# A chunk's gate and up halves handed over separately, and the low half of h subtracted on GpSimd

## The chip, the cores and the metric

The kernel runs on one core of a Trainium2 chip. The metric is the device time of one execution in microseconds (us), the median of several runs. The core has a matrix engine (TensorE, PE in the profile), VectorE (DVE), ScalarE (ACT), GpSimd (POOL) and a queue that issues transfers (SyncE, SP). Each engine takes its own instructions strictly in order; they meet only at semaphores.

## The reference, cut to what matters

```python
low, highs = x, []                                  # x: (2, 4096, 512)
for _ in range(2):                                  # two levels of a filter bank along the tokens
    highs.append(dwconv(low, g_filter)[:, ::2]); low = dwconv(low, h_filter)[:, ::2]
low = linear_attention(low, 16)
for h in reversed(highs):
    low = dwconv(repeat(low, 2), h_synth) + dwconv(repeat(h, 2), g_synth)
x = layernorm(x + layer_norm(x + low, gamma, beta))

gate = x @ (w_gate / 127).T                         # w_gate, w_up: (1536, 512)
up   = x @ (w_up / 127).T
h    = silu(gate) * up
x    = layernorm(x + h @ (w_down / 127).T)
```

The last four lines are the feed-forward part (FFN). Each float operand of its products is carried as two float16 halves: a high half, which is the value rounded to float16, and a low half, which is the value less its high half.

## The kernel before, in words

After an opening (the first analysis of the filter bank, up to 203 us of the span) the program runs eight iterations of 1024 tokens. An iteration does the FFN of its tokens in two blocks of 512 tokens (b is 0 or 1), and beside it, in small steps, the filter bank, the attention and the layer norms of the next iteration; iterations 0 to 2 also do a piece of the analysis of the second batch ("ANA"), and the last has no next one. The table `BESIDE` (line 66) says which step stands beside which chunk: `(b, k)` with k from 0 to 11 for the gate and up chunks, and from 12 to 15 for the four groups of tokens of the down product. On each engine the order is written out by these loops; nothing reorders it.

A chunk k is 128 of the 1536 hidden columns. For it

- PE (`gate_up`, L512 to L524) waits until the product of chunk k-2 has been formed (`h_mul`; that frees the PSUM buffers `ps_gu[k % 2]`), then runs 8 matmuls for gate and 8 for up, and signals once, `gu_ready`, after all 16.
- ACT (L752 to L759) waits for `gu_ready`, writes silu(gate) to `gate_s` (L754), does its "early" steps of the table, waits for the product, writes the high half `h_hi` (L758, a cast to float16), and does its "late" steps. The squares of the layer norms are among the late ones (`norm1q` L671, `normq` L677) and so is `normx` (L683).
- DVE (L1064 to L1080) waits for the silu, multiplies it by the up half, from PSUM, into `h_f` (L1070), does its steps of the table, waits for `h_hi` and writes the low half, `h_f - h_hi` (L1076, `hid<-h_f,hid` in the profile). For k = 0 the steps stand ahead of the product, for k = 11 after the low half.
- POOL has no part in a chunk. It does small steps of the layer norms on one value in each partition (`norm1` L795, `norm1q` L803 and L806, `norm2` L810, `normq` L816 to L821) and `xbeta` (L790), an addition of two SBUF tiles of 128x512.

The filter steps on DVE are `scalar_tensor_tensor` instructions, all recorded at L864: `low1` and `high1` are six of 514 elements and two short corrections of edges (L869), `synth1a` and `synth1b` five of 512, `synth2` eight of 257 and an edge. All their tensor operands lie in SBUF, as those of `norm2` (L1006, L1012) do. The product (L1070), `x_lo` (L1020), `att` (L941) and the residual `z` (L1088) read one operand from PSUM and one from SBUF.

The layer norm of a group t of 128 tokens goes round the engines: DVE `norm2` (L1006, L1012), then POOL L810, then ACT's square L677, then POOL L816 to L821, then ACT `normx` L683, then PE's transposes L507, ACT `x_hi` L688, and DVE `x_lo` L1020.

## Time and profile before

| | |
|---|---|
| median of 3 runs | 1384.56 us (1384.21, 1384.56, 1386.04) |
| profiled execution, first to last instruction | 1382.5 us |
| granted PE clock, mean | 0.971 of full; 1.00 in every stretch from 350 us to 1250 us |
| PE, DVE, ACT, POOL busy | 1245.5, 988.1, 688.8, 373.0 us |
| iterations 0 to 7 | from 203 us to the end; 155 us each for 1 and 2, 144.4 us each for 4, 5 and 6 |

The span is the profiled execution's own time; the median of the runs lies 2.1 us above it. A matmul of 512 columns is recorded with 380 ns, but at full clock one starts every 0.216 us, and its record overlaps the next one's; so an idle stretch of PE of g us in the profile stands for g + 0.16 us in which no matmul started. A chunk of 16 matmuls takes 3.46 us when nothing holds it.

### The profile page before, as it was taken

To read this page: it belongs to the slowest core of one execution; us is meant where nothing else is said; L and a number is where in the kernel's file an instruction comes from. 1 tells how busy PE (TensorE), PEld (TensorE's weight loads), DVE (VectorE), ACT (ScalarE), POOL (GpSimd) and SP (SyncE) were. 2 spreads that over 40 slices of the span, in tenths; PEclk is the share of its full clock that TensorE was granted. 3 is DMA by queue.
4 is the path that set the end of the run, shared out by engine and by line. 5 is a ranking of instruction groups with operands and counts; after the bars stand their busy time and mean duration, and the time that the engine had idled before them with its cause. 6 is when DMAs were issued, how large, how long until landed. Compare 5 with 4: busy or idle time off the path is not lost.

```text
span 1382.5 us, 18903 instructions
## 1 busy us (share of the span) xinstructions
PE 1245.5 (90%) x5920; PEld 629.5 (46%) x5920; DVE 988.1 (71%) x1913; ACT 688.8 (50%) x1384; POOL 373.0 (27%) x790
## 2 busy tenths in 40 slices
PE   3997039998999989998999999999999999999998
PEld 3885025444444444444544444444444444444443
DVE  2677938988688958988489738883898478854332
ACT  2663046345753466346753466346634664365432
POOL 2001033133423044223413143304321341234101
PEclk9998559999999999999999999999999999999999
DMA  8963033000520014000500041002200130010000
GB/s 262 285 238 123 0 123 108 23 24 24 176 77 31 0 55 147 20 23 24 176 16 31 8 148 30 31 1 84 100 23 8 53 122 23 15 38 24 16 16 31
DMA packets 48465, 95.20 MB, mean 69 GB/s; under 512 B 8448, under 2 KB 25088, under 8 KB 47376
## 3 DMA queue, kind: packets, MB, share of 16 engines
q1 hardware_dynamic: 48400, 94.42, 20.8%
q8 instruction: 30, 0.49, 0.1%
q14 instruction: 35, 0.29, 0.1%
HBM read 69.21 MB, written 25.19 MB: 68 GB/s over the span
## 4 chain that ended last, share of the span: by engine, by line
DVE 29%; PE 27%; issue 22%; ACT 12%; POOL 9%; SPq 0%; DMA 0%; DVEq 0%; POOLq 0%; ACTq 0%
DVE s_chan L864 6%; DVE h_f L1070 5%; DVE low L864 5%; PE ps_down L540 3%; PE ps_down L539 3%; PE ps_gate L522 3%; PE ps_gate L523 3%; PE ps_up L523 3%; PE ps_up L522 3%; DVE hid L1076 3%; POOL rs L819 3%; DVE h_mem L864 3%; PE ps_down L572 2%; ACT junk L671 2%; DVE l L864 2%
## 5 line engine op out<-in xcount | busy, mean ns | idle before, releaser
L522 PE MATMUL ps_gate<-x_hi,w 128*128 128x512 f16 x768 | 292.4, 381 | 27.5 <-DVE h_f L1070 25.4
L539 PE MATMUL ps_down<-w,hid 128*128 128x512 f16 x768 | 292.1, 380 | 0.1
L540 PE MATMUL ps_down<-w,hid 128*128 128x512 f16 x768 | 292.1, 380 | 0.0
L523 PE MATMUL ps_gate<-x_lo,w 128*128 128x512 f16 x768 | 292.0, 380 | 0.0
L522 PE MATMUL ps_up<-x_hi,w 128*128 128x512 f16 x768 | 291.1, 379 | 0.0
L523 PE MATMUL ps_up<-x_lo,w 128*128 128x512 f16 x768 | 291.1, 379 | 0.0
L758 ACT ACTIVATE hid<-h_f 128x512 f16<-128x512 f32 x192 | 121.0, 630 | 203.2 <-DVE h_f L1070 203.2
L1070 DVE SCALAR_TENSOR_TENSOR h_f<-ps_up,gate_s 128x512 f32<-128x512 f32 x192 | 131.7, 686 | 123.7 <-ACT gate_s L754 123.1
L1076 DVE TENSOR_TENSOR hid<-h_f,hid 128x512 f16<-128x512 f32 x192 | 139.3, 725 | 57.7 <-ACT hid L758 56.8
L754 ACT ACTIVATE gate_s<-ps_gate 128x512 f32<-128x512 f32 x192 | 112.1, 584 | 70.0 <-PE ps_up L523 69.8
L522 PEld LDWEIGHTS ps_gate<-x_hi,w 128*128 128x128 f16 x768 | 75.2, 98 | 124.9 <-DVE h_f L1070 42.2
L522 PEld LDWEIGHTS ps_up<-x_hi,w 128*128 128x128 f16 x768 | 75.2, 98 | 90.8 <-issue 0.3
L523 PEld LDWEIGHTS ps_up<-x_lo,w 128*128 128x128 f16 x768 | 75.1, 98 | 90.8 <-issue 0.3
L790 POOL TENSOR_TENSOR xt<-xt,beta_b 128x512 f32<-128x512 f32 x64 | 90.1, 1429 | 97.6 <-DMA xt<-x_tok 96.8
L539 PEld LDWEIGHTS ps_down<-w,hid 128*128 128x128 f16 x768 | 75.3, 98 | 86.8 <-DVE z L1088 3.5
L540 PEld LDWEIGHTS ps_down<-w,hid 128*128 128x128 f16 x768 | 75.3, 98 | 85.2 <-issue 1.1
L864 DVE SCALAR_TENSOR_TENSOR s_chan<-low,coef,s_chan 128x512 f32<-128x512 f32 x160 | 111.5, 748 | 1.1
L523 PEld LDWEIGHTS ps_gate<-x_lo,w 128*128 128x128 f16 x768 | 75.3, 98 | 78.7 <-issue 0.8
L795 POOL TENSOR_TENSOR rs<-rs,minus_part 128x1 f32<-128x1 f32 x64 | 21.2, 331 | 324.6 <-ACT x L666 324.6
L1020 DVE TENSOR_TENSOR x_lo<-ps_y,x_hi 128x512 f16<-128x512 f32 x64 | 43.9, 687 | 85.2 <-ACT x_hi L688 85.2
L746 ACT ACTIVATE z<-z,rs 128x512 f32<-128x512 f32 x64 | 52.0, 812 | 83.3 <-POOL rs L821 83.3
L741 ACT ACTIVATE junk<-z,rs 128x512 f16<-128x512 f32 x64 | 46.0, 718 | 89.9 <-POOL rs L839 89.9
(106 smaller groups left out, 1803.8 us busy)
## 6 DMA issues: line engine op xcount, KB each, us to landing
xa<-x_chan SPq DMA_DIRECT2D x32, 515.0 KB, 5.6
xb<-x_chan SPq DMA_DIRECT2D x8, 2060.0 KB, 8.9
xt<-x_tok SPq DMA_DIRECT2D x64, 256.0 KB, 2.6
out<-z SPq DMA_DIRECT2D x64, 256.0 KB, 2.0
hid<-weights SPq DMA_DIRECT2D x12, 768.0 KB, 6.7
q_in<-q_scratch SPq DMA_DIRECT2D x8, 518.0 KB, 8.5
h_in<-h_scratch SPq DMA_DIRECT2D x8, 518.0 KB, 9.5
h_scratch<-h SPq DMA_DIRECT2D x8, 512.0 KB, 9.2
```

The lines of the kernel that those rows point to most:

```text
L522: pe.matmul(ps_gu[k % 2][g][:, :], w, x1_hi[:, b, c, :], start=(c == 0), stop=False)
L523: mm = pe.matmul(ps_gu[k % 2][g][:, :], w, x1_lo[:, b, c, :], start=False, stop=(c == NC - 1))
L539: pe.matmul(ps_d[t % 2][:, :], h_hi[:, k, t * P:(t + 1) * P], w, start=(k == 0), stop=False)
L540: mm = pe.matmul(ps_d[t % 2][:, :], h_lo[:, k, t * P:(t + 1) * P], w, start=False, stop=(k == NH - 1))
L741: nc.scalar.activation(junk[:, :], z[:, t, :], ACT.Square, bias=rs3[:, t, 1:2], accum_out=rs3[:, t, 2:3]).then_inc(z_squares, 1)
L746: nc.scalar.activation(z[:, t, :], z[:, t, :], ACT.Identity, bias=rs3[:, t, 5:6], scale=rs3[:, t, 4:5]).then_inc(out_done, 1)
L754: nc.scalar.activation(gate_s[:, k % 2, :], ps_gu[k % 2][0][:, :], ACT.Silu, scale=WSCALE / X1_SCALE).then_inc(silu_done, 1)
L758: nc.scalar.activation(h_hi[:, k, :], h_f[:, k % 2, :], ACT.Copy).then_inc(hi_done, 1)
L790: nc.gpsimd.tensor_tensor(xt[:, t % 4, :], xt[:, t % 4, :], beta_b[:, :], ALU.add).then_inc(x_beta, 1)
L864: return V.scalar_tensor_tensor(out=acc, in0=src, scalar=coef[:, c, n:n + 1], in1=acc if add is None else add, op0=ALU.mult, op1=ALU.add)
L1070: V.scalar_tensor_tensor(out=h_f[:, k % 2, :], in0=ps_gu[k % 2][1][:, :], scalar=WSCALE * H_SCALE / X1_SCALE, in1=gate_s[:, k % 2, :], op0 ...
L1076: V.tensor_tensor(h_lo[:, k, :], h_f[:, k % 2, :], h_hi[:, k, :], ALU.subtract).then_inc(lo_done, 1)
```

## The change

Four things are changed together.

1. PE signals the gate half and the up half of a chunk apart (`gate_ready`, `up_ready`). Ahead of the gate half it waits for the silu of chunk k-2, ahead of the up half for the product of chunk k-2.
2. ACT's silu waits for `gate_ready`, and for the low half of chunk k-4.
3. The silu is written into `h_f`, a ring of four buffers, and DVE writes the product over it; `gate_s` is gone. DVE waits for the silu and for `up_ready`, and its steps of the table follow the product in every chunk but the first.
4. The low half is subtracted on POOL (L840 of the changed kernel). Of POOL's steps of a chunk `norm1` stands ahead of it, and `norm1q`, `xbeta`, `norm2` and `normq` behind it. Since POOL first waits for `h_hi` of the chunk, it can't be ahead of ACT's copy any more.

```diff
+RING = 4
...
-        gate_s = sb("gate_s", [P, 2, BLK])
-        h_f = sb("h_f", [P, 2, BLK])
+        h_f = sb("h_f", [P, RING, BLK])
...
-                pe.wait_ge(h_mul, NH * B + k + 1)
                 for g in range(2):
+
+                    pe.wait_ge((silu_done, h_mul)[g], NH * B + k + 1)
                     for c in range(NC):
...
-                mm.then_inc(gu_ready, 1)
+                    mm.then_inc((gate_ready, up_ready)[g], 1)
...
-                        act.wait_ge(gu_ready, NH * B + k + 1)
-                        nc.scalar.activation(gate_s[:, k % 2, :], ps_gu[k % 2][0][:, :], ACT.Silu,
+                        act.wait_ge(gate_ready, NH * B + k + 1)
+                        act.wait_ge(lo_done, NH * B + k + 1)
+                        nc.scalar.activation(h_f[:, k % RING, :], ps_gu[k % 2][0][:, :], ACT.Silu,
...
+            early = {"norm1": norm1}
+            late = {"norm1q": norm1q, "xbeta": xbeta, "norm2": norm2, "normq": normq}
...
-                        beside(b, k, i, batch, analysis, last, steps)
+                        beside(b, k, i, batch, analysis, last, early)
+                        if k < NH:
+                            pool.wait_ge(hi_done, NH * (2 * i + b) + k + 1)
+                            nc.gpsimd.tensor_tensor(h_lo[:, k, :], h_f[:, k % RING, :], h_hi[:, k, :], ALU.subtract
+                                                    ).then_inc(lo_done, 1)
+                        beside(b, k, i, batch, analysis, last, late)
...
+            V.memset(h_f[:, 1, 0:1], 0.0).then_inc(silu_done, 2)
+            V.memset(h_f[:, 1, 1:2], 0.0).then_inc(lo_done, RING)
...
-                        dve.wait_ge(silu_done, n + 1)
-                        V.scalar_tensor_tensor(out=h_f[:, k % 2, :], in0=ps_gu[k % 2][1][:, :],
-                                               scalar=WSCALE * H_SCALE / X1_SCALE, in1=gate_s[:, k % 2, :],
+                        dve.wait_ge(silu_done, n + 3)
+                        dve.wait_ge(up_ready, n + 1)
+                        V.scalar_tensor_tensor(out=h_f[:, k % RING, :], in0=ps_gu[k % 2][1][:, :],
+                                               scalar=WSCALE * H_SCALE / X1_SCALE, in1=h_f[:, k % RING, :],
                                                op0=ALU.mult, op1=ALU.mult).then_inc(h_mul, 1)
-                        if 0 < k < NH - 1:
-                            beside(b, k, i, batch, analysis, last, steps)
-                        dve.wait_ge(hi_done, n + 1)
-                        V.tensor_tensor(h_lo[:, k, :], h_f[:, k % 2, :], h_hi[:, k, :], ALU.subtract
-                                        ).then_inc(lo_done, 1)
-                        if k == NH - 1:
-
+                        if k > 0:
                             beside(b, k, i, batch, analysis, last, steps)
```

The PE waits of the down product for the low halves (L534, L537) are raised by RING, since that semaphore now starts at 4.

How POOL's row stands in block 1, chunks 4 to 8. Before, from the end of block 0 (L819 and L821 are its last norm) to the first norm of block 1:

```order
L819 TENSOR_TENSOR rs<-rs,minus_half 128x1
L821 TENSOR_TENSOR rs<-rs 128x1
L789 ISA
L790 TENSOR_TENSOR xt<-xt,beta_b 128x512 x4
L794 ISA
L795 TENSOR_TENSOR rs<-rs,minus_part 128x1
```

And now, from the low half of chunk 5 (L793 is `xbeta`, L840 the low half; L839 and L792 set up waits):

```order
L840 TENSOR_TENSOR hid<-h_f,hid 128x512
L792 ISA
L793 TENSOR_TENSOR xt<-xt,beta_b 128x512
L839 REGISTER_ALU
L840 TENSOR_TENSOR hid<-h_f,hid 128x512
L793 TENSOR_TENSOR xt<-xt,beta_b 128x512
L839 REGISTER_ALU
L840 TENSOR_TENSOR hid<-h_f,hid 128x512
L793 TENSOR_TENSOR xt<-xt,beta_b 128x512
```

The four `xbeta` could run as soon as their data had landed; now each stands behind the low half of its own chunk, 5 to 8.

POOL in block 0, chunks 6 and 7. Before (L795 `norm1` 7, L803 and L806 `norm1q` 7, L810 `norm2` 6, L816 to L821 `normq` 6):

```order
L795 TENSOR_TENSOR rs<-rs,minus_part 128x1
L803 TENSOR_SCALAR rs<-rs 128x1
L806 TENSOR_TENSOR rs<-rs,minus_half 128x1
L810 TENSOR_TENSOR rs<-rs,minus_part 128x1
L816 TENSOR_SCALAR rs<-rs 128x1
L819 TENSOR_TENSOR rs<-rs,minus_half 128x1
L821 TENSOR_TENSOR rs<-rs 128x1
L810 TENSOR_TENSOR rs<-rs,minus_part 128x1
```

And now (the same lines are L798, L806, L809, L813, L819, L822 and L824):

```order
L798 TENSOR_TENSOR rs<-rs,minus_part 128x1
L839 REGISTER_ALU
L840 TENSOR_TENSOR hid<-h_f,hid 128x512
L806 TENSOR_SCALAR rs<-rs 128x1
L809 TENSOR_TENSOR rs<-rs,minus_half 128x1
L813 TENSOR_TENSOR rs<-rs,minus_part 128x1
L819 TENSOR_SCALAR rs<-rs 128x1
L822 TENSOR_TENSOR rs<-rs,minus_half 128x1
L824 TENSOR_TENSOR rs<-rs 128x1
L839 REGISTER_ALU
L840 TENSOR_TENSOR hid<-h_f,hid 128x512
L813 TENSOR_TENSOR rs<-rs,minus_part 128x1
```

The low half of a chunk now stands ahead of the norm steps of that chunk.

DVE in block 1, chunks 2 and 3 (L864 is `synth1b`, L1070 the product, L1076 the low half). Before:

```order
L1070 SCALAR_TENSOR_TENSOR h_f<-ps_up,gate_s 128x512
L991 REGISTER_ALU
L864 SCALAR_TENSOR_TENSOR s_chan<-low,coef,s_chan 128x512 x5
L1076 TENSOR_TENSOR hid<-h_f,hid 128x512
L1069 REGISTER_ALU
L1070 SCALAR_TENSOR_TENSOR h_f<-ps_up,gate_s 128x512
L941 TENSOR_TENSOR att<-ps_x,att 128x259
```

And now (L1083 is the product, L876 `synth1b`):

```order
L1083 SCALAR_TENSOR_TENSOR h_f<-ps_up,h_f 128x512
L1003 REGISTER_ALU
L876 SCALAR_TENSOR_TENSOR s_chan<-low,coef,s_chan 128x512 x5
L1081 REGISTER_ALU
L1083 SCALAR_TENSOR_TENSOR h_f<-ps_up,h_f 128x512
L953 TENSOR_TENSOR att<-ps_x,att 128x259
```

The low half is gone from between the filter steps and the next product; nothing else moved there.

## Rows read from the trace of the kernel before

**Rows 1.** The page's part 1: busy us, share of the span, instructions.

```profile
PE 1245.5 (90%) x5920; PEld 629.5 (46%) x5920; DVE 988.1 (71%) x1913; ACT 688.8 (50%) x1384; POOL 373.0 (27%) x790
```

**Rows 2.** Busy by stretch (PE, PEld, DVE, ACT, POOL): an early, a middle, the last iteration.

```profile
512.60:658.00 145.40, 135.74 (x653) 65.16 (x654) 125.41 (x243) 78.07 (x161) 47.48 (x85) 1.00 0.17 53
...
947.00:1091.00 144.00, 139.64 (x664) 66.15 (x664) 106.07 (x194) 73.69 (x152) 43.15 (x95) 1.00 0.15 51
1248.00:1382.00 134.00, 128.08 (x609) 60.01 (x608) 47.68 (x83) 56.21 (x107) 25.13 (x68) 0.99 0.05 20
```

**Rows 3.** Waits from 200 us on: engine, line, releaser; total us, times, longest.

```profile
PE ps_gate L522 <- DVE h_f L1070: 25.4, 36, 1.4
...
PE ps_y L507 <- DVE x_lo L1020: 16.2, 11, 2.6
...
PE ps_x L489 <- ACT x L666: 3.0, 3, 1.0
```

**Rows 4.** Timeline of PE, iteration 5: start, us, line, tiles [idle before, releaser].

```profile
995.43 0.39 PE L522 MATMUL ps_gate<-x_hi,w 128*128 128x512 f16 x1 [0.29 <-DVE h_f L1070]
...
999.59 0.39 PE L522 MATMUL ps_gate<-x_hi,w 128*128 128x512 f16 x1 [0.53 <-DVE h_f L1070]
...
1051.48 0.39 PE L522 MATMUL ps_gate<-x_hi,w 128*128 128x512 f16 x1 [0.71 <-DVE h_f L1070]
...
1056.52 0.39 PE L522 MATMUL ps_gate<-x_hi,w 128*128 128x512 f16 x1 [1.41 <-DVE h_f L1070]
```

**Rows 5.** The page's part 5: busy, mean ns, idle before and releaser.

```profile
L1070 DVE SCALAR_TENSOR_TENSOR h_f<-ps_up,gate_s 128x512 f32<-128x512 f32 x192 | 131.7, 686 | 123.7 <-ACT gate_s L754 123.1
L1076 DVE TENSOR_TENSOR hid<-h_f,hid 128x512 f16<-128x512 f32 x192 | 139.3, 725 | 57.7 <-ACT hid L758 56.8
...
L790 POOL TENSOR_TENSOR xt<-xt,beta_b 128x512 f32<-128x512 f32 x64 | 90.1, 1429 | 97.6 <-DMA xt<-x_tok 96.8
```

**Rows 6.** Timelines of POOL and DVE where an addition of POOL meets filter steps.

```profile
117.15 5.92 POOL L790 TENSOR_TENSOR xt<-xt,beta_b 128x512 f32<-128x512 f32 x4 [96.85 <-DMA xt<-x_tok]
114.31 5.12 DVE L864 SCALAR_TENSOR_TENSOR h_mem<-xb,coef,h_mem 128x514 f32<-128x514 f32 x6
980.49 4.07 DVE L864 SCALAR_TENSOR_TENSOR h_mem<-xb,coef,h_mem 128x514 f32<-128x514 f32 x6
367.61 1.27 POOL L790 TENSOR_TENSOR xt<-xt,beta_b 128x512 f32<-128x512 f32 x1
367.79 1.65 DVE L1006 SCALAR_TENSOR_TENSOR x<-x,rs,gamma_b 128x512 f32<-128x512 f32 x1
```

**Rows 7.** Timeline of DVE, iteration 5, block 1, chunks 0 to 8.

```profile
1038.19 0.69 DVE L1070 SCALAR_TENSOR_TENSOR h_f<-ps_up,gate_s 128x512 f32<-128x512 f32 x1 [1.41 <-ACT gate_s L754]
1039.58 1.48 DVE L1076 TENSOR_TENSOR hid<-h_f,hid 128x512 f16<-128x512 f32 x1 [0.70 <-ACT hid L758]
...
1046.70 3.52 DVE L864 SCALAR_TENSOR_TENSOR s_chan<-low,coef,s_chan 128x512 f32<-128x512 f32 x5
1050.14 0.68 DVE L1076 TENSOR_TENSOR hid<-h_f,hid 128x512 f16<-128x512 f32 x1
1050.74 0.68 DVE L1070 SCALAR_TENSOR_TENSOR h_f<-ps_up,gate_s 128x512 f32<-128x512 f32 x1
...
1055.78 0.68 DVE L1070 SCALAR_TENSOR_TENSOR h_f<-ps_up,gate_s 128x512 f32<-128x512 f32 x1
...
1069.03 0.68 DVE L1070 SCALAR_TENSOR_TENSOR h_f<-ps_up,gate_s 128x512 f32<-128x512 f32 x1
```

**Rows 8.** Timeline of ACT, iteration 5, block 0: square, silu of chunk 7, silu of 8.

```profile
992.73 0.72 ACT L677 ACTIVATE junk<-x,rs 128x512 f16<-128x512 f32 x1 [1.80 <-POOL rs L810]
993.45 0.57 ACT L754 ACTIVATE gate_s<-ps_gate 128x512 f32<-128x512 f32 x1
...
998.23 0.58 ACT L754 ACTIVATE gate_s<-ps_gate 128x512 f32<-128x512 f32 x1
```

**Rows 9.** Timeline of POOL, iteration 1, block 1, chunk 10, among `band2` steps of DVE.

```profile
481.72 1.70 POOL L803 TENSOR_SCALAR rs<-rs 128x1 f32<-128x1 f32 x1 [2.08 <-ACT junk L671]
```

17 lines of the change are left out of this document (9 added, 8 removed).

## The prediction

> **What bounds the kernel now.** I read first the busy shares on the page [rows 1]: PE is busy 90% of the span, DVE 71%, POOL 27%. Then the same by stretch [rows 2]. In a middle iteration PE is busy 139.6 of 144 us and DVE 106.1; in an early one PE 135.7 of 145.4 and DVE 125.4; in the last, which has no next iteration beside it, DVE 47.7 of 134. So PE sets the pace, and DVE has spare time on the average but little in the early iterations. What is to be had is what PE stands idle. The list of waits gives it [rows 3]: 25.4 us in 36 waits for the product of chunk k-2, and 16.2 and 3.0 us for the layer norms. Each wait costs 0.16 us more than it shows, since a matmul's record overlaps the next one's, so the 36 waits are worth 25.4 + 36 x 0.16 = 31 us. They stand in the same places in every iteration. In iteration 5 there are four [rows 4]: in block 0 ahead of chunks 9 and 10 (0.29 and 0.53, that is 1.1 us with the overlap), in block 1 ahead of chunks 5 and 6 (0.71 and 1.41, that is 2.4 us).
>
> **What the change removes.** DVE loses 192 low halves. The product behind one starts 0.60 us after it (1050.14, 1050.74) [rows 7], so 192 x 0.61 = 117 us of work, and DVE also waited 57.7 us for the high half [rows 5]: 175 us. That is the case for the change. Handing over gate and up apart is free on every engine (one more signal, one more wait) and gives PE slack: the wait for the product moves from the gate half to the up half, 8 x 0.216 = 1.73 us later, and the silu no longer stands between the end of the up half and the product, which is worth up to 0.6 us more. Against the waits of rows 4, the longest of which is 1.41 + 0.16 = 1.6 us, this alone would be enough to remove them, as long as DVE's products come no later than now. The ring of four costs nothing that I can find: the silu of chunk k waits for a low half four chunks back, some 14 us earlier, and two memsets are added ahead of the opening.
>
> **What it adds, and why it isn't free.** POOL gets 192 subtractions of two SBUF tiles. The nearest row is its own addition of the same size, L790: 1.27 us when nothing is in its way [rows 6], 1.43 on the mean with what is [rows 5]. I take 1.27, with 1.1 and 1.5 as bounds (one operand and the output are float16 here, which no row of POOL shows). 192 x 1.27 = 244 us; POOL has room for it.
>
> But POOL and DVE exclude each other. The rows that show it [rows 6]: six filter steps of DVE take 4.07 us, and took 5.12 where the additions of POOL fell on them; there POOL's four took 5.92 instead of 4 x 1.27 = 5.1. The `norm2` step that started 0.18 us after an addition of POOL took 1.65 us instead of 0.75. And a product (one operand from PSUM) that fell within additions of POOL took its usual 0.69 (1038.19) [rows 7]. So a DVE instruction with two SBUF operands and a POOL instruction with two run one after the other, each whole, and where both are waiting they take turns. A subtraction that becomes ready in the middle of filter steps therefore costs DVE 1.27 us, twice the 0.61 that it cost as DVE's own. Only where DVE stands idle, or does a product, is it free. In a chunk with filter steps it never is: the high half is ready 0.8 us after the product's end, and the steps last 3.4 to 4.2 us.
>
> The Trainium skill (GPSIMD Engine Reference, section 3.1) gives 4497 ns for a `tensor_tensor` of 2048 elements, so as an estimate by that page 1.12 us for 512; the row says 1.27. By 1.12 each term for the low halves below would be about a tenth smaller; the sum goes by the row.
>
> **Block 1, chunks 1 to 10** (iteration 5, times on its clock) [rows 7]. `synth1b` takes 3.44 us (1046.70 to 1050.14), a product 0.61, `att` and `synth2` what is left between the products at 1050.74 and 1055.78, 5.04 - 2 x 0.61 = 3.8. The product of chunk 1 comes at 1040.1 instead of 1040.99, since no locked-out low half (1.48) stands ahead of it. Then each chunk with filter steps gets 1.27 instead of 0.61: products of chunks 2, 3, 4 at 1046.2, 1051.5, 1057.5 (the last was at 1055.78). PE would reach the up half of chunk 6 at 1055.8 with no waits at all, and now waits for the product of chunk 4 until 1058.1: 2.3 us. The product of chunk 5 waits for the silu (59.4), and the low half of chunk 4 hides there. Behind it come `synth1b`, the low half of 5, and now also an `xbeta`, which before ran in DVE's idle time around 1038: 0.6 + 3.4 + 1.3 + 1.3 puts product 6 at 1066.1, and PE's up half of chunk 8 waits 1.7 us. Product 7 at 1068.0; then `synth1b` again, taking turns with two `xbeta` and the low half of 7 (the low half of 6 hides): product 8 at 1076.0 instead of 1069.03, and the up half of chunk 10 waits 3.0 us. Together 7.0 us where there were 2.4: **+4.6 us**.
>
> **Block 0, chunks 5 to 10.** DVE has `high1` (4.07 us and two edges) [rows 6] behind products 4 and 6. One and a third `xbeta` (1.7) and the low half of 4 (1.27 for 0.61) fall into the first, which itself starts 0.4 later: product 5 comes 2.8 us later, which costs PE 0.8. The larger part goes through ACT [rows 8]. Before, ACT's square L677 of `normq` waited for POOL's L810 until 992.73, and only behind it, in ACT's order, at 993.45, comes the silu of chunk 7. Now POOL must first wait for the high half of chunk 6, get its turn (up to 0.66) and subtract (1.27) before it comes to `norm1q`, `norm2` and `normq`, and all of it starts 3.1 us later because product 6 does. I get the silu of chunk 7 at 998.2 instead of 993.45, and PE's gate half of chunk 9, which now waits for it, 3.0 us late; and once more for the silu of chunk 8 (now 998.23), 2.0 us. Together 5.8 where there were 1.1: **+4.7 us**. Queued behind the waiting POOL are all layer-norm steps, behind the waiting ACT the silu, and behind that both PE and DVE.
>
> **The sum.** Iterations 0 to 6 have both places: 7 x (4.6 + 4.7) = 65 us. In iterations 0 to 2 DVE also has `band2` beside chunks 8 to 12 of block 1 and no idle time to catch up in; four low halves at 0.66 more, an `xbeta` of 1.27 and the lateness left from chunk 8 (2 us) make 6 us each, bounded by 0 and 8: +18. Against that the 16.2 + 3.0 us of layer-norm waits [rows 3] may vanish where PE comes late itself: -19, bounded by 0. 65 + 18 - 19 = +64 us. The profiled span is 1382.5, the runs lie 2.1 above it: 1384.6 + 64 = **1448 us**. The down product and the last iteration I cost at nothing: DVE does no low halves in the first, and stands idle 65% of the second.
>
> **Rivals.**
> 1. *The slack is enough* (faster). If the low halves mostly fell into DVE's idle time (123.1 us of waits for the silu [rows 5]), the products would come no later, and the 31 us of waits would go: 1353, or anything up to 1381 if only part goes. For it: DVE gets 175 us back, more than half of the 244. Against it: the idle time isn't where PE waits.
> 2. *Cushioned* (a little slower). The turns go so that most low halves start beside a product or `x_lo` and cost DVE 0.67 instead of 1.27, and the `xbeta` find idle time: then the two places lose about 1.5 us each instead of 4.6, 7 x 3 = 21, less some of the layer-norm waits: 1388 to 1410.
> 3. *POOL is passed over.* One row speaks of it [rows 9]: an instruction that takes 0.19 us took 1.70 among short steps of DVE and ended only when a product came. If that were the rule, the low halves would cost DVE nothing in a run, but POOL's norm steps would be held behind them to the run's end, 3 to 4 us, and with them ACT's squares and the silu. At two places of 7 iterations, 3 to 5 us each, less the 31: 1395 to 1425. The rows at 117 us speak against it: POOL got its turn after each step. The Trainium skill (SBUF — State Buffer, section Who interferes with whom) says that whoever issues first has the shared pair for the whole instruction and knows no passing over; by it the sum stands.
> 4. *No difference*: gains and losses cancel, 1382 to 1387. Nothing in the rows asks for that.
>
> **Chances.** A difference under 0.2% (2.8 us) can't be told from none. The forecast's own case, 1410 to 1490: 60%. Rivals 2 and 3 together 18%. Faster 16%. The same 6%. The range from 1385 to 1485 leaves out the faster case and a little above.
>
> **What would show it.** In the changed profile: POOL's low half at 1.27 us alone and more on the mean; DVE's L864 steps longer on the mean (now 747 ns for 512 elements); PE waiting in the up half for the product, and in the gate half for the silu, in total some 60 to 100 us, in block 0 around chunks 7 to 10 and in block 1 around chunks 6 to 10; ACT's L677 waiting longer for POOL. The last iteration should take what it takes now. I am wrong if the filter steps keep their length beside POOL's subtractions, if POOL's subtraction is well under 1 us, or if the silu isn't late behind the squares.

## The result and the profile after

The changed kernel takes 1450.0 us (median of 4 runs, 1447.3 to 1450.4) against 1384.4 us before (1384.1 to 1386.0): ratio 1.047, 95% interval 1.046 to 1.049. The profiled execution has a span of 1448.5 us, against 1382.5.

The page of the changed kernel, parts 1 and 5, against [rows 1, 5]. L840 is GpSimd's new subtraction, L793 its x + beta step, L876 the filter steps (L864 before), L1083 the product, L757 the silu, L524 the gate and up matmuls.

```profile
PE 1263.0 (87%) x5920; PEld 633.6 (44%) x5920; DVE 985.8 (68%) x1723; ACT 687.0 (47%) x1384; POOL 616.4 (43%) x982
...
L840 POOL TENSOR_TENSOR hid<-h_f,hid 128x512 f16<-128x512 f32 x192 | 251.7, 1311 | 308.1 <-ACT hid L761 307.9
...
L1083 DVE SCALAR_TENSOR_TENSOR h_f<-ps_up,h_f 128x512 f32<-128x512 f32 x192 | 131.9, 687 | 225.7 <-ACT h_f L757 169.9
...
L876 DVE SCALAR_TENSOR_TENSOR s_chan<-low,coef,s_chan 128x512 f32<-128x512 f32 x160 | 151.7, 998 | 1.1
L793 POOL TENSOR_TENSOR xt<-xt,beta_b 128x512 f32<-128x512 f32 x64 | 96.0, 1502 | 97.0 <-DMA xt<-x_tok 97.0
```

The same filter steps in the kernel before:

```profile
L864 DVE SCALAR_TENSOR_TENSOR s_chan<-low,coef,s_chan 128x512 f32<-128x512 f32 x160 | 111.5, 748 | 1.1
```

The first thing to see is what did not change: DVE has 190 instructions fewer and is busy 985.8 us, against 988.1. The records of its neighbouring instructions overlap by up to 0.1 us, so the 139.3 us of its subtractions [rows 5] can't simply be taken off. Counted over all records but those of the subtractions, DVE was busy 867.0 us before: 121 us went with them, and its other instructions are busy 119 us longer now. These filter steps on `s_chan` take 998 ns on the mean instead of 748.

The waits from 200 us on, first of PE, then of ACT (engine, line, releaser: us in total, times, longest), against [rows 3]:

```profile
PE ps_gate L524 <- ACT h_f L757: 21.7, 22, 1.6
PE ps_x L490 <- DVE s_chan L876: 20.5, 7, 3.0
PE ps_y L508 <- DVE x_lo L1032: 18.9, 12, 2.8
PE ps_up L524 <- DVE h_f L1083: 10.0, 14, 1.0
PE ps_x L490 <- ACT x L668: 8.1, 3, 4.0
PE ps_x L435 <- ACT h_mem L634: 7.8, 4, 3.1
PE ps_x L443 <- ACT h_mem L634: 6.7, 4, 2.4
...
ACT junk L679 <- POOL rs L813: 90.1, 53, 2.8
```

The wait of the gate half for the product (25.4 us) is gone. In its place stand three: the gate half for the silu, the up half for the product, and, not there before, the transposes of the next iteration's first layer norm (L490) for the last filter run. The last three waits of PE in the list stand in iterations 0 to 3; the same three took 5.2 us before, and 22.6 now. All of PE's waits together went from 48.9 us in 58 to 97.1 us in 74.

Where they stand in the same iteration as [rows 4], now at 992 to 1145 us, from PE's timeline. The first two are the gate halves of chunks 9 and 10 of block 0, the next two the up halves of chunks 6 and 8 of block 1, then the transposes ahead of chunk 10:

```profile
1044.90 0.39 PE L524 MATMUL ps_gate<-x_hi,w 128*128 128x512 f16 x1 [1.63 <-ACT h_f L757]
...
1049.69 0.39 PE L524 MATMUL ps_gate<-x_hi,w 128*128 128x512 f16 x1 [1.16 <-ACT h_f L757]
...
1106.96 0.39 PE L524 MATMUL ps_up<-x_hi,w 128*128 128x512 f16 x1 [0.67 <-DVE h_f L1083]
...
1114.78 0.39 PE L524 MATMUL ps_up<-x_hi,w 128*128 128x512 f16 x1 [0.74 <-DVE h_f L1083]
...
1123.08 0.65 PE L490 MATMUL ps_x<-ident,s_chan 128*128 128x128 f32 x4 [2.95 <-DVE s_chan L876]
```

How the silu comes late, from the timeline of POOL and, in the second fence, of ACT. POOL subtracts the low half of chunk 6 (1040.24), only then comes to its norm steps, and those last longer than their 0.19 and 0.55 us among DVE's filters. L813 (1043.18) lets ACT's square L679 go, and behind that in ACT's order stands the silu (1044.27) for which the gate half at 1044.90 waits:

```profile
1040.24 1.34 POOL L840 TENSOR_TENSOR hid<-h_f,hid 128x512 f16<-128x512 f32 x1 [1.08 <-ACT hid L761]
1041.67 0.52 POOL L806 TENSOR_SCALAR rs<-rs 128x1 f32<-128x1 f32 x1
1042.27 0.94 POOL L809 TENSOR_TENSOR rs<-rs,minus_half 128x1 f32<-128x1 f32 x1
1043.18 0.34 POOL L813 TENSOR_TENSOR rs<-rs,minus_part 128x1 f32<-128x1 f32 x1
```

```profile
1043.55 0.72 ACT L679 ACTIVATE junk<-x,rs 128x512 f16<-128x512 f32 x1 [2.68 <-POOL rs L813]
1044.18 0.18 ACT L679 ACTIVATION_READ_ACCUMULATOR junk<-x,rs 128x1 f32 x1
1044.27 0.57 ACT L757 ACTIVATE h_f<-ps_gate 128x512 f32<-128x512 f32 x1
```

How the filters of block 1 get longer, from DVE's timeline and, in the second fence, POOL's, against [rows 7]: the run of five steps takes 3.52 us alone, 4.42 with one subtraction in it (POOL's at 1097.10), 5.43 with a subtraction and an x + beta (1109.52, 1111.07), and 6.44 with a subtraction and two x + beta (the run at 1116.51, for which the transposes at 1123.08 wait).

```profile
1096.27 4.42 DVE L876 SCALAR_TENSOR_TENSOR s_chan<-low,coef,s_chan 128x512 f32<-128x512 f32 x5
...
1108.69 5.43 DVE L876 SCALAR_TENSOR_TENSOR s_chan<-low,coef,s_chan 128x512 f32<-128x512 f32 x5
...
1116.51 6.44 DVE L876 SCALAR_TENSOR_TENSOR s_chan<-low,coef,s_chan 128x512 f32<-128x512 f32 x5
```

```profile
1097.10 1.60 POOL L840 TENSOR_TENSOR hid<-h_f,hid 128x512 f16<-128x512 f32 x1 [4.04 <-ACT hid L761]
...
1109.52 1.59 POOL L840 TENSOR_TENSOR hid<-h_f,hid 128x512 f16<-128x512 f32 x1 [0.72 <-ACT hid L761]
1111.07 1.71 POOL L793 TENSOR_TENSOR xt<-xt,beta_b 128x512 f32<-128x512 f32 x1
```

And one thing that is no wait. Two stretches of the changed kernel (from, to, length, busy PE, PEld, DVE, ACT, POOL, granted clock, DMA share, GB/s):

```profile
1140.00:1144.00 4.00, 2.99 (x14) 1.18 (x12) 0.00 (x0) 2.93 (x8) 1.40 (x6) 1.00 0.28 66
1145.40:1148.80 3.40, 3.40 (x12) 1.53 (x13) 1.81 (x5) 2.41 (x6) 1.42 (x5) 0.58 0.00 0
```

Behind the wait for norm3 (2.33 us, ended at 1145.33) the granted clock falls to its lower level for 3.4 us: eight matmuls start 0.43 us apart instead of 0.215, which costs 1.7 us. Counted over the timeline from 200 us on, 74 gate, up and down matmuls run so in the changed kernel and 16 before: 58 x 0.215 = 12 us of the growth, an estimate. In iterations 3 to 6 each fall comes right behind the norm3 wait of block 1; iterations 0 to 2 have some at other places too (at 327, 508 and 654 us). With the waits (97.1 - 48.9 us, and 16 more overlaps of 0.16) that makes 63 of the 66 us.

The growth by iteration, from the ends of PE's norm3 wait in block 1 (345.16, 500.44, ... 1235.95 before; 354.50, 518.97, ... 1298.90 after): +8.3 for the first, then 9.2, 8.3, 8.9, 9.1, 9.0, 9.1, and +3.1 for the last; the opening adds 1.0. Sum 66.

### The profile page after: what moved, and what is told of

It reads as the page before. It is cut to its first block, busy times and chain, and to the rows that moved or that the text cites. A ratio compares the mean times of both kernels' runs of the same rounds, so it can differ in the third digit from the quotient of the medians.

```text
span 1448.5 us, 19419 instructions
## 1 busy us (share of the span) xinstructions
PE 1263.0 (87%) x5920; PEld 633.6 (44%) x5920; DVE 985.8 (68%) x1723; ACT 687.0 (47%) x1384; POOL 616.4 (43%) x982
## 4 chain that ended last, share of the span: by engine, by line
issue 27%; DVE 23%; PE 22%; POOL 17%; ACT 9%; SPq 0%; DMA 0%; POOLq 0%; DVEq 0%; ACTq 0%
DVE s_chan L876 7%; POOL hid L840 6%; PE ps_down L541 5%; PE ps_down L542 5%; DVE low L876 3%; DVE h_f L1083 3%; DVE h_mem L876 3%; POOL rs L822 2%; POOL xt L793 2%; PE ps_down L574 2%; ACT h_f L757 2%; PE ps_gate L524 2%; DVE l L876 1%; PE ps_gate L525 1%; PE ps_up L525 1%
## 5 line engine op out<-in xcount | busy, mean ns | idle before, releaser
L840 POOL TENSOR_TENSOR hid<-h_f,hid 128x512 f16<-128x512 f32 x192 | 251.7, 1311 | 308.1 <-ACT hid L761 307.9
L524 PE MATMUL ps_gate<-x_hi,w 128*128 128x512 f16 x768 | 294.1, 383 | 23.3 <-ACT h_f L757 21.7
L524 PE MATMUL ps_up<-x_hi,w 128*128 128x512 f16 x768 | 291.8, 380 | 10.1 <-DVE h_f L1083 10.0
L541 PE MATMUL ps_down<-w,hid 128*128 128x512 f16 x768 | 297.7, 388 | 1.9 <-POOL hid L840 1.9
L542 PE MATMUL ps_down<-w,hid 128*128 128x512 f16 x768 | 297.1, 387 | 0.0
L1083 DVE SCALAR_TENSOR_TENSOR h_f<-ps_up,h_f 128x512 f32<-128x512 f32 x192 | 131.9, 687 | 225.7 <-ACT h_f L757 169.9
L876 DVE SCALAR_TENSOR_TENSOR s_chan<-low,coef,s_chan 128x512 f32<-128x512 f32 x160 | 151.7, 998 | 1.1
L793 POOL TENSOR_TENSOR xt<-xt,beta_b 128x512 f32<-128x512 f32 x64 | 96.0, 1502 | 97.0 <-DMA xt<-x_tok 97.0
L524 PEld LDWEIGHTS ps_gate<-x_hi,w 128*128 128x128 f16 x768 | 75.7, 99 | 115.2 <-ACT h_f L757 33.0
L524 PEld LDWEIGHTS ps_up<-x_hi,w 128*128 128x128 f16 x768 | 75.3, 98 | 107.7 <-DVE h_f L1083 18.5
L757 ACT ACTIVATE h_f<-ps_gate 128x512 f32<-128x512 f32 x192 | 111.5, 581 | 6.4 <-PE ps_gate L525 6.4
L819 POOL TENSOR_SCALAR rs<-rs 128x1 f32<-128x1 f32 x128 | 33.5, 262 | 140.2 <-ACT junk L743 72.6
L490 PE MATMUL ps_x<-ident,s_chan 128*128 128x128 f32 x256 | 42.4, 291 | 56.8 <-DVE s_chan L876 45.8
```

The source lines that it names most:

```text
L524: pe.matmul(ps_gu[k % 2][g][:, :], w, x1_hi[:, b, c, :], start=(c == 0), stop=False)
L541: pe.matmul(ps_d[t % 2][:, :], h_hi[:, k, t * P:(t + 1) * P], w, start=(k == 0), stop=False)
L542: mm = pe.matmul(ps_d[t % 2][:, :], h_lo[:, k, t * P:(t + 1) * P], w, start=False, stop=(k == NH - 1))
L757: nc.scalar.activation(h_f[:, k % RING, :], ps_gu[k % 2][0][:, :], ACT.Silu, scale=WSCALE / X1_SCALE).then_inc(silu_done, 1)
L793: nc.gpsimd.tensor_tensor(xt[:, t % 4, :], xt[:, t % 4, :], beta_b[:, :], ALU.add).then_inc(x_beta, 1)
L840: nc.gpsimd.tensor_tensor(h_lo[:, k, :], h_f[:, k % RING, :], h_hi[:, k, :], ALU.subtract).then_inc(lo_done, 1)
```

## The experiments

Every kernel was timed beside the kernel before; ratios are to it. The last column is the mean length of a middle iteration (the mean of three, between the norm3 transposes in block 1 of iterations 3 to 6).

```
kernel                               us      ratio (95%)              middle iteration
before                               1384.4                           144.4
changed                              1450.0  1.047 (1.046 to 1.049)   153.5
e1  hand-over alone                  1376.1  0.995 (0.994 to 0.997)   142.7
e2  subtraction on GpSimd alone      1451.2  1.048 (1.047 to 1.050)   153.4
e8  GpSimd subtracts in block 0      1401.3  1.013 (1.012 to 1.015)   146.8
e8  GpSimd subtracts in block 1      1424.3  1.029 (1.028 to 1.031)   149.2
e4  fill instead of subtraction      1354.9  0.980 (0.978 to 0.981)   140.8
e9  longer fill                      1375.9  0.994 (0.992 to 0.996)   143.2
e4  one tile read                    1434.7  1.037 (1.035 to 1.039)   151.2
e5  subtraction behind norm steps    1468.5  1.062 (1.060 to 1.064)   157.0
e5b the same in chunks 0 to 8        1439.6  1.040 (1.038 to 1.041)   153.4
e7  all low halves a chunk late      1406.9  1.017 (1.015 to 1.018)   146.9
e7b the same, last one early         1381.5  0.998 (0.997 to 0.999)   143.5
e10 one low half moved               1373.0  0.991 (0.990 to 0.993)   142.1
```

### The two parts of the change apart

e1, the hand-over without the move (the subtraction back on VectorE, in its old place; the ring of four stays):

```
-                        if k < NH:
-                            pool.wait_ge(hi_done, NH * (2 * i + b) + k + 1)
-                            nc.gpsimd.tensor_tensor(h_lo[:, k, :], h_f[:, k % RING, :], h_hi[:, k, :], ALU.subtract
-                                                    ).then_inc(lo_done, 1)
...
-                        if k > 0:
+                        if 0 < k < NH - 1:
                             beside(b, k, i, batch, analysis, last, steps)
+                        dve.wait_ge(hi_done, n + 1)
+                        V.tensor_tensor(h_lo[:, k, :], h_f[:, k % RING, :], h_hi[:, k, :], ALU.subtract
+                                        ).then_inc(lo_done, 1)
+                        if k == NH - 1:
+                            beside(b, k, i, batch, analysis, last, steps)
```

> The changed kernel with the low half's subtraction back on VectorE, in its old place: the separate hand-over of gate and up and the ring stay, nothing is left out. Theory (the subtraction on GpSimd carries the whole loss, the hand-over is a gain): TensorE's waits for VectorE's product before a chunk (25 us in the kernel before) go and nothing takes their place, 1350 to 1370 us, GpSimd's steps and VectorE's filter instructions as short as before (filter instructions on s_chan near 750 ns). Rival (handing the gate half over against the silu, and writing the product over it, costs something by itself): 1385 us or more.

1376.1 us (1371.7 to 1378.1): between the two. The direction of the theory holds, the size doesn't. Waits of PE from 200 us on:

```profile
PE ps_y L508 <- DVE x_lo L1026: 16.6, 10, 2.6
PE ps_x L490 <- ACT x L668: 8.0, 3, 2.7
PE ps_down L541 <- DVE z L1094: 4.9, 7, 0.7
PE ps_up L524 <- DVE h_f L1077: 3.5, 7, 0.6
```

The waits of the gate half for the product are gone, but PE, which now runs ahead, meets the next late thing: the down product waits for `z` (0.70 an iteration), the up half of chunk 6 for product 4 (0.56), norm3 waits 0.18 longer. In a middle iteration four waits, 2.94 us in all, and four overlaps of 0.16 went, 3.6 us, and 0.70 + 0.56 + 0.18 and two overlaps, 1.8 us, came: 1.8 us are left of it, and 144.42 - 142.65 is 1.8. One thing has to be kept apart: the profiled execution of e1 is the fastest of its four (1371.7), and its opening ended 6.2 us earlier than that of the kernel before (194.08 against 200.26 us), for a reason that stays open. From there to the end the two take 1175.8 and 1182.2 us: the loop itself gains 6.4 us.

e2, the move without the hand-over (silu and product still share the ring of four):

```
+                pe.wait_ge(h_mul, NH * B + k + 1)
                 for g in range(2):
-                    pe.wait_ge((silu_done, h_mul)[g], NH * B + k + 1)
...
-                        act.wait_ge(gate_ready, NH * B + k + 1)
+                        act.wait_ge(up_ready, NH * B + k + 1)
```

> The changed kernel with one hand-over again: TensorE waits for the product before all 16 matmuls of a chunk and signals once, behind them; the subtraction stays on GpSimd, nothing is left out. Theory (in the changed kernel the slack of 1.7 us a chunk given by the hand-over still absorbs part of VectorE's lateness): the waits before the gate half come on top, 1465 to 1495 us. Rival (the hand-over is worth nothing any more since other chains end last): 1446 to 1454 us.

1451.2 us, the rival. The move costs 67 us by itself; the hand-over is worth 6 to 8 us before it and about nothing behind it.

### Block by block

The edit for block 0; for block 1 the two conditions change places.

```
-                        if k < NH:
+                        if k < NH and b == 0:
...
+                        if b == 1:
+                            dve.wait_ge(hi_done, n + 1)
+                            V.tensor_tensor(h_lo[:, k, :], h_f[:, k % RING, :], h_hi[:, k, :], ALU.subtract
+                                            ).then_inc(lo_done, 1)
...
```

> The changed kernel with the low halves on GpSimd in the first block of an iteration alone (b = 0), and on VectorE, in their old place, in the second; nothing is left out. The hand-over with all low halves on VectorE took 1376.1 us, with all on GpSimd 1450.0. Theory (each block pays its own part: in the first it is the silus behind norm steps and the filters on h_mem, read from the trace as some 4 to 5 us an iteration): 1376 + 8 x 5 = 1416 us, 1408 to 1424. Rival (the two blocks cost only together, since what one gives the other absorbs it): under 1390 or over 1440.

> The changed kernel with the low halves on GpSimd in the second block of an iteration alone (b = 1), and on VectorE in the first; nothing is left out. Theory (the second block pays for the run of filters before products 6, 8 and 10, for the transposes that wait for the last synthesis step, for the late norm3 and for the fall of TensorE's clock behind it, together some 4 to 5 us an iteration): 1376 + 8 x 4.5 = 1412 us, 1404 to 1420, with the fall of the clock still there. Rival (it is the first block that lengthens everything, the second only inherits its lateness): under 1390.

Against the hand-over alone, block 0 costs 25 us and block 1 48, together 73.5; both at once cost 73.9. So the costs add, as expected, but the shares were expected about equal and are one to two, each time just outside its expected range. From the end of the opening on, the profiled executions say the same: 24.9 and 46.1 us more than e1, and 71.4 with both. PE's largest wait in the kernel with GpSimd in block 0:

```profile
PE ps_gate L524 <- ACT h_f L757: 19.3, 19, 1.6
```

and the three largest in the kernel with GpSimd in block 1:

```profile
PE ps_x L490 <- DVE s_chan L876: 20.5, 7, 3.0
PE ps_y L508 <- DVE x_lo L1032: 18.2, 11, 2.6
PE ps_up L524 <- DVE h_f L1083: 11.9, 14, 1.1
```

Block 0 pays mainly with the silu (and in the early iterations with a wait at L435, 8.1 us where e1 has 0.5), block 1 with the filters, and it brings most of the clock's falls: 76 matmuls at the lower level, against 38 with block 0 alone and 17 in the hand-over alone.

### Hold or queue

GpSimd's operation does two things: it holds VectorE's two-tile instructions off, and it stands ahead of the layer norms' steps in GpSimd's own order. Three kernels keep its place, waits and signals and change what it does; each has a tiny operation on one value in each partition ahead of the large one. The low half is left out of the down product in all three (its matmuls run, on zeros).

```
                         if k < NH:
                             pool.wait_ge(hi_done, NH * (2 * i + b) + k + 1)
-                            nc.gpsimd.tensor_tensor(h_lo[:, k, :], h_f[:, k % RING, :], h_hi[:, k, :], ALU.subtract
+                            pool.wait_ge(spared, NH * (2 * i + b) + k + 1)
+                            nc.gpsimd.tensor_tensor(tiny[:, :], minus_half[:, :], minus_part[:, :], ALU.mult
+                                                    ).then_inc(spared, 1)
+                            nc.gpsimd.memset(h_lo[:, k, :], 0.0).then_inc(lo_done, 1)
```

> The changed kernel with GpSimd's subtraction replaced by a tiny operation and a fill of the low half with zeros, in the same place of GpSimd's queue and with the same waits and signals: GpSimd reads no large tile there. Left out: the low half of h in the down product (its matmuls still run, on zeros). Theory (most of the loss is VectorE's instructions held for 0.90 us by every subtraction): filter instructions on s_chan fall back from 998 to near 750 ns and the time to 1365 to 1400 us. Rival (the loss is GpSimd's queue, with the layer norms' steps behind the subtraction and the silu behind them): still above 1425 us, since GpSimd's place in the order is the same.

The longer fill adds one operation ahead of the fill:

```
+                            pool.wait_ge(spared2, NH * (2 * i + b) + k + 1)
+                            nc.gpsimd.tensor_tensor(tiny2[:, :], minus_half[:, :], minus_part[:, :], ALU.mult
+                                                    ).then_inc(spared2, 1)
                             nc.gpsimd.memset(h_lo[:, k, :], 0.0).then_inc(lo_done, 1)
```

> As the kernel with the fill (1354.9 us), with a second tiny operation ahead of the fill, so that GpSimd is busy for about 0.36 + 0.36 + 0.52 = 1.24 us a chunk, near the 1.31 us of the subtraction, while VectorE is held for only 0.25 us a chunk as with the fill. Left out: the low half of h in the down product. Theory (the hold on VectorE carries most of the loss; 1.3 us more in GpSimd's queue are mostly slack): 1355 to 1385 us. Rival (it is GpSimd's queue, with the norm steps behind it; the kernel that read one tile took 1434.7 us with 2.07 us a chunk and little hold): 1395 to 1430 us, with the waits of the gate halves for the silu back.

And the third kernel reads `h_f` in place of the fill:

```
-                            nc.gpsimd.memset(h_lo[:, k, :], 0.0).then_inc(lo_done, 1)
+                            nc.gpsimd.tensor_scalar(h_lo[:, k, :], h_f[:, k % RING, :], 0.0, None, ALU.mult).then_inc(lo_done, 1)
```

> As the kernel with the fill, but the large operation on GpSimd multiplies h_f by zero: one tile of 128x512 is read, one written. Left out: the low half of h in the down product. It should last near the 1.16 us of the subtraction, or half of that. Theory A (GpSimd holds VectorE only when it reads two tiles): VectorE's filter instructions as short as with the fill (863 ns on s_chan or less) and the time near the fill's 1355 us, 1350 to 1365, even if the operation lasts over 1 us; that would also show that the length of GpSimd's queue costs little. Theory B (any reading of that size holds VectorE): filters of 950 ns or more and 1400 us or more.

What the operations take, lines of the groups by line (busy, mean ns of one), first of the kernel with the fill:

```profile
L846 POOL MEMSET hid<- 128x512 f16 x192 | 100.4, 523 | 0.0
...
L844 POOL TENSOR_TENSOR tiny<-minus_half,minus_part 128x1 f32<-128x1 f32 x192 | 68.9, 359 | 334.3 <-ACT hid L763 333.5
```

of the kernel with the longer fill, its two tiny operations:

```profile
L849 POOL TENSOR_TENSOR tiny<-minus_half,minus_part 128x1 f32<-128x1 f32 x192 | 77.7, 405 | 0.0
...
L846 POOL TENSOR_TENSOR tiny<-minus_half,minus_part 128x1 f32<-128x1 f32 x192 | 66.3, 345 | 294.5 <-ACT hid L764 294.1
```

and of the kernel that reads one tile:

```profile
L846 POOL TENSOR_SCALAR hid<-h_f 128x512 f16<-128x512 f32 x192 | 328.8, 1712 | 0.0
```

These means give 0.88 us of GpSimd for a chunk (fill), 1.27 (longer fill), 1.31 (subtraction) and 2.05 (one tile read), but the records overlap here too. From the start of the tiny operation to the end of the large one it is 0.82, 1.16, 1.31 and 2.01 us on the mean. The times are 1355, 1376, 1450 and 1435: the fill came out faster than its theory, the longer fill within its own, and the kernel that reads one tile fits neither of its two, with filter steps on `s_chan` of 839 ns as in theory A and a time as in theory B.

Two comparisons. Between the two fills nothing differs but 0.35 us of queue a chunk, and that costs 21 us; PE's waits of the gate half for the silu go from 1.4 to 8.9 us. The longer fill fills the queue nearly like the subtraction (1.16 and 1.31 us) and holds nothing; of the 74 us between them, the missing 0.15 us a chunk are worth some 9 at the price between the fills, so that the hold has 65 to 74, an estimate. Reading one tile, with 0.85 us a chunk more than the longer fill and a small hold, costs 59 on top of it. So the theory was right that the hold is the larger part, and wrong that the queue has slack: a microsecond a chunk in GpSimd's order costs some 60 us by this estimate, since norm steps, squares and silus hang on it. It isn't the zeros in the down product that make the fills fast: the third kernel multiplies zeros too.

The rows for the hold, from the timelines of DVE and then of POOL; the first two fences are of the kernel with the fill, the last two of the kernel that reads one tile:

```profile
1025.62 3.54 DVE L881 SCALAR_TENSOR_TENSOR s_chan<-low,coef,s_chan 128x512 f32<-128x512 f32 x5
...
1036.25 4.53 DVE L881 SCALAR_TENSOR_TENSOR s_chan<-low,coef,s_chan 128x512 f32<-128x512 f32 x5
```

```profile
1027.03 0.52 POOL L846 MEMSET hid<- 128x512 f16 x1
...
1038.12 1.32 POOL L795 TENSOR_TENSOR xt<-xt,beta_b 128x512 f32<-128x512 f32 x1
```

```profile
1085.16 3.87 DVE L881 SCALAR_TENSOR_TENSOR s_chan<-low,coef,s_chan 128x512 f32<-128x512 f32 x5
```

```profile
1086.58 2.00 POOL L846 TENSOR_SCALAR hid<-h_f 128x512 f16<-128x512 f32 x1
```

A fill within a filter run leaves it at 3.54 us: it holds nothing. Still DVE is busier in the fill kernel (893.8 us) than in e1 without its subtractions (865.2, counted over all other records): 29 us. Of these some 23 lie in DVE instructions that met an x + beta step, which the wait for the copy has moved among the filters (4.53 with one of them). My expectation for the longer fill took 47 us for this, by setting 138.8 off against 985.4, and put them down to the fills, 0.25 us each; both were wrong, and the longer fill makes DVE no busier than the fill (893.3). In the changed kernel DVE is 121 us busier than 865.2; if what the fill kernel shows is there too, 29 us, the subtractions take 92.

### The order on GpSimd

```
                         beside(b, k, i, batch, analysis, last, early)
+                        beside(b, k, i, batch, analysis, last, late)
                         if k < NH:
                             ...
-                        beside(b, k, i, batch, analysis, last, late)
```

> The changed kernel with GpSimd's subtraction of a chunk put behind all layer-norm and x + beta steps of that chunk rather than ahead of most of them; nothing is left out. Theory of the queue (the silu's waits in the first eleven chunks of block 0, some 4 us an iteration, come from norm steps that stand behind the subtraction): these waits shrink and the time falls by 15 to 30 us, to 1420 to 1435. Rival (VectorE held by the lock is the cause there too, wherever the subtraction stands): 1445 to 1455 us.

1468.5 us, slower than either theory gave: the down product now waits 35.4 us in 14 waits for the last low halves of a block, which stand behind norm steps. The second kernel keeps the old order in chunks 9 to 11:

```
                         beside(b, k, i, batch, analysis, last, early)
-                        beside(b, k, i, batch, analysis, last, late)
+                        if k < NH - 3:
+                            beside(b, k, i, batch, analysis, last, late)
                         if k < NH:
                             ...
+                        if k >= NH - 3:
+                            beside(b, k, i, batch, analysis, last, late)
```

> The changed kernel with the subtraction behind the norm steps of its chunk in chunks 0 to 8 of each block, and ahead of them, as in the changed kernel, in chunks 9 to 11, where the down product waits for it. Nothing is left out. Theory (with the subtraction behind all steps it was the down product's wait for it, 35 us, that took the gain; the waits for the silu come from the queue): 1450 less some 10 to 25 us, 1425 to 1440. Rival (what comes later now meets other filter steps and the next chunk's norms, so that the order on GpSimd is worth nothing): 1445 to 1460.

1439.6 us, 10 less than the changed kernel, at the weak end of the range. The gate halves' waits for the silu fall from 21.7 to 14.9 us, the up halves' rise from 10.0 to 17.9, and the wait of L490 stays at 20.5 to the tenth. The middle iterations gained nothing by this exchange (153.4 against 153.5 us). What fell are the three waits of the early iterations (L490 for ACT, L435, L443), from 22.6 to 12.5 us. So the queue's order matters a little, and not where the theory looked; neither of the two orders tried makes up for the hold. Whether a better place exists for every single chunk was not tried.

### Towards a faster kernel

With the subtraction on VectorE the ring of four allows it to be late. e7 puts each one chunk later, behind the next product and ahead of the filters:

```
-                        if 0 < k < NH - 1:
+                        if k > 0:
+                            dve.wait_ge(hi_done, n)
+                            V.tensor_tensor(h_lo[:, k - 1, :], h_f[:, (k - 1) % RING, :], h_hi[:, k - 1, :],
+                                            ALU.subtract).then_inc(lo_done, 1)
                             beside(b, k, i, batch, analysis, last, steps)
+                        if k == NH - 1:
                             ...
-                        if k == NH - 1:
-                            beside(b, k, i, batch, analysis, last, steps)
```

The low half of chunk 11 itself, the last of a block, stays in its own chunk, behind the steps.

> The hand-over with all low halves on VectorE, each subtracted one chunk later, straight behind the next product and ahead of the filter steps; the ring of four makes room. Nothing is left out. The 57 us in which VectorE stood before the subtractions for ScalarE's copy go. Theory (VectorE's lateness still decides some of TensorE's waits): a little faster than the hand-over alone at 1376.1, 1362 to 1374 us. Rival (the filters now start 0.72 us later, behind the old subtraction, and what follows them is late instead): 1376 to 1386 us.

1406.9 us, worse than both: the last low half of a block stood behind its chunk's norm steps, the down product waited for it (the first of PE's waits, below), and 79 matmuls ran at the lower clock.

```profile
PE ps_down L541 <- DVE hid L1087: 23.9, 7, 3.5
```

The next kernel puts that one ahead of the norm steps:

```
+                        if k == NH - 1:
+                            dve.wait_ge(hi_done, n + 1)
+                            V.tensor_tensor(h_lo[:, k, :], h_f[:, k % RING, :], h_hi[:, k, :], ALU.subtract
+                                            ).then_inc(lo_done, 1)
+                        if k > 0:
                             beside(b, k, i, batch, analysis, last, steps)
-                        if k == NH - 1:
-                            ...
```

> All low halves on VectorE, each one chunk late, straight behind the next product and ahead of the filter steps, and now the last one of a block ahead of the norm steps too, where before it stood behind them and the down product waited 3.5 us for it. Nothing is left out. Theory (that wait and the fall of TensorE's clock behind it were the 31 us that the delayed version lost against the hand-over alone): 1406.9 - 7 x 3.5 - 10 = 1372 us, 1366 to 1378, no slower than the hand-over alone at 1376.1. Rival (delaying the filters by 0.72 us costs by itself): over 1380.

1381.5 us (1381.0 to 1382.0): the 25 us are recovered, but it stays 5 us above the hand-over alone, as the rival said. About 2 us of the 5 are in the loop (1178.1 us from the end of the opening to the end, against 1175.8 in e1), how much of the rest is the opening, which ended at 201.6 us here and at 194.1 in e1, the runs don't say. The work ahead of the late product 4 of block 1 is the same, only another chunk's subtraction; and the filters start 0.6 us later everywhere. So the last kernel moves only the one subtraction that stands ahead of that product:

```
+                        if b == 1 and k == 4:
+                            dve.wait_ge(hi_done, n)
+                            V.tensor_tensor(h_lo[:, k - 1, :], h_f[:, (k - 1) % RING, :], h_hi[:, k - 1, :],
+                                            ALU.subtract).then_inc(lo_done, 1)
...
+                        if not (b == 1 and k == 3):
```

> The hand-over with all low halves on VectorE, and one of the 24 low halves of an iteration moved: that of chunk 3 of the second block, which stood between the long filter run of chunk 3 and product 4, now follows product 4. Nothing is left out. In the hand-over alone (1376.1 us) the up half of chunk 6 there waits 0.56 us for product 4 in each of seven iterations; the subtraction ahead of that product took 0.72 us. Theory (a low half costs where it stands ahead of a late product, and only there): those waits go and nothing else comes, 1376.1 - 7 x 0.56 = 1372 us, 1370 to 1374. Rival (the wait is a symptom, and the time comes back at the next late chain, as when all were delayed): 1375 to 1380.

1373.0 us, 0.991 of the kernel before, by its median the fastest kernel here with the whole computation, and as expected. Its interval (0.990 to 0.993) lies just below that of the hand-over alone (0.994 to 0.997), but one of e1's four executions, the profiled one, took 1371.7. What settles it is the loop, from the end of the opening to the end: 1170.1 us in this kernel, 1175.8 in e1, 1182.2 in the kernel before. PE's waits from 200 us on:

```profile
PE ps_y L508 <- DVE x_lo L1026: 15.3, 11, 1.8
PE ps_x L490 <- ACT x L668: 8.0, 3, 2.7
PE ps_down L541 <- DVE z L1099: 4.9, 7, 0.7
PE ps_x L443 <- ACT h_mem L634: 2.8, 2, 1.4
PE ps_gate L524 <- ACT h_f L757: 2.6, 3, 0.9
```

The up half for the product (3.5 us in 7 in e1) no longer stands among them, nothing has come in its place, and a middle iteration is 0.5 us shorter (142.12 against 142.65). Of the 5.7 us of the loop 1.6 lie in the three middle iterations; the rest lies in iterations 0 to 3 and wasn't followed up.

## Why the prediction was right, and where it was not

The forecast was 1448.0, the result 1450.0. The sign and the mechanism were right; the sum is made of terms of which several were off and cancelled.

**GpSimd's subtraction.** Forecast 1.27 us alone, from x + beta. The rows give 1.16 alone (105 of the 192 show 1.15 or 1.16) and 1.31 on the mean. The estimate by the Trainium skill (GPSIMD Engine Reference, section 3.1) was 1.12: the rows are nearer to that than to my nearest row.

**The hold.** The step that carries the forecast, and it stood: e9 puts it at 65 to 74 us. The size was too large: 0.90 us for a subtraction in a filter run (4.42 - 3.52), not 1.27, since the hold is shorter than the instruction. The product of chunk 4 came 0.09 us later relative to its block than before where 1.7 was forecast, those of chunks 6 and 8 by 1.3 and 3.5 where 3.7 and 7.0 were. The Trainium skill (SBUF — State Buffer, section Who interferes with whom) says for a VectorE instruction in a 2-port mode that whoever issues first holds the shared pair for the whole instruction, and in its section Summary: rules for kernel authors the same for one with two SBUF inputs beside a GpSimd instruction that reads SBUF. By that, as an estimate, a filter run would grow by all of the 1.16 us, and it grew by 0.90. The section Who interferes with whom also says that VectorE's two-input instructions don't contend with a GpSimd instruction that only writes SBUF: the trace of the fill agrees, with 3.54 us.

**The removal from DVE.** I counted 117 us of work as taken off DVE, and 121 went. The hold I set against it place by place; in sum it is plainer: 119 us came back.

**Block 1, forecast +4.6 an iteration.** The up halves of chunks 6 and 8 wait 0.67 and 0.74 (forecast 2.3 and 1.7). Chunk 10's forecast wait of 3.0 for product 8 didn't come, because PE stopped earlier, for 2.95, at L490, which is queued ahead of it and needs the same filter run. With the overlaps 4.8 us where there were 2.4: +2.4. Right in cause, half in size.

**Block 0, forecast +4.7.** The chain POOL, square, silu is there as described. The waits are 1.63 and 1.16 at chunks 9 and 10 (forecast 3.0 and 2.0) and 0.33, 0.72, 0.36 and 0.25 at places that I had not named: 5.4 us with the overlaps, where there were 1.3 (the 1.1 and an idle 0.16 that the forecast left out): +4.1.

**Not in the sum.** The norm3 wait of block 1 grew by 0.8 an iteration. And the clock: 1.7 an iteration, behind that wait. 2.4 + 4.1 + 0.8 + 1.7 = 9.0, and the middle iterations grew by 9.1. Before, the clock fell so behind the norm3 wait at 345.16 (2.56 us), but not behind those of 2.56 and 2.63 at 500 and 655, nor behind those of 1.55; so I could have named it as a risk, not as a term.

**The correction for iterations 0 to 2 (+18) and for the layer-norm waits (-19).** The early iterations grew by 8.3 to 9.2 us, like the rest, so in sum the +18 didn't come. But they grew differently. At the place that I named, beside `band2`, the wait of L490 for ACT took 4.0 us in iteration 1 instead of 1.0, and in the three iterations together 8.1 instead of 3.0; the waits for ACT's `h_mem` (L435, L443), which I hadn't looked at, grew from 2.2 to 12.4 us. Against that the silu and up waits took 3.8 us an iteration there, and 5.2 to 5.4 in iterations 4 to 6. The norm waits grew instead of vanishing. I had both terms with their bounds at zero, and they cancelled. That the sum came within 2 us of the result is luck to this extent: the two places of a middle iteration gave 6.5 us where I had 9.3, and norm3 and the clock, not in the sum, gave 2.5.

**The last iteration, forecast 0.** +3.1 us: block 0's waits for the silu are there too (1.0 us in two), since its norm steps are, and one of 0.36 for `x_lo`, together 1.8 with the overlaps; and the clock falls once more, right behind the norm3 wait that ends at 1298.90, for about 1.7.

**The hand-over.** The step that failed most: I wrote that alone it would remove 31 us of waits. e1 gives 7 or 8 (6.4 in the loop), since half of what a wait gives up is taken by the next late thing, and some of what is gained is given back in the early iterations (L490 for ACT: 8.0 us in three waits, before 3.0). In the forecast itself the error was small, as there the slack was set against waits that were larger than it; e2 shows that the hand-over is worth nothing beside the subtraction on GpSimd.

**The signs.** I had looked for 60 to 100 us of waits of the gate half for the silu and the up half for the product. They are 21.7 + 10.0 = 31.7 us, 37 with the overlaps; another 20.5 stand at L490, and the rest of the growth is norm3, the early waits and the clock. So the total was reached in part by waits that I had not named.

**The rivals.** Passed over (3) has something in it: POOL's norm steps do get longer among the filters (0.94 instead of 0.55 at 1042.27), but the subtractions get their turn. What would have shown me wrong (filters at their old length, a subtraction under 1 us, silus on time) didn't occur.

## What to carry to other kernels

Work moved from VectorE to GpSimd that reads two large SBUF tiles isn't taken off VectorE where VectorE itself is running on two tiles: look at what DVE does in the microsecond in which the moved work becomes ready, not at its idle share. Ask as well what stands behind it in GpSimd's order. And a wait that is removed is worth at most its distance to the next late thing on the same engine; a step costs where it stands ahead of a late product, so move that one and leave the rest (here that was worth 3 us at the medians).

## What the runs showed of the hardware

- A GpSimd subtraction of two 128x512 tiles (float32, float16, to float16) took 1.16 us alone and cost a run of VectorE's two-tile steps 0.90; a multiplication of one 128x512 tile took 1.49 us alone, 2.00 in such a run, and cost the run 0.35; a fill of 128x512 float16 took 0.52 us in every place and cost it nothing.
- GpSimd's operations on 128x1 suffer by their surroundings still more, for their length: 0.19 us alone and up to 0.75 beside VectorE's steps in the changed kernel (up to 1.70 in the kernel before); the power, 0.55 alone and up to 0.96 (1.08 before).
- The granted clock fell to the lower level for about 3 us, mostly eight matmuls, and once for twice as long, once or twice in each of the iterations 0 to 6 of the changed kernel (2.33 us idle ahead of it at 1145 us, PE busy 2.99 of 4.00 us a little earlier), once in the whole loop of the kernel before: 12 us of the 66. It is about as much of e7's loss (79 matmuls at the lower level, 21 to 23 in e7b and e10). What decides it stays open: before, waits of 2.56 us were followed by a fall once and not another time.
